# Top-k read: chosen probabilities by exp(scores) minus exp(scores without the chosen), subtracted on GpSimd

## What is computed

```python
# x: (16, 64, 256), the query rows; ctx_1024: (16, 1601, 256), the memory rows
q = query @ Wq.T + bq
k = mem_state @ Wk.T + bk
v = mem_state @ Wv.T + bv
scores = jnp.einsum('btd,bsd->bts', q, k) * scale
vals, idx = jax.lax.top_k(scores, top_k)              # top_k = 32 of s = 1601
masked = jnp.full_like(scores, -jnp.inf)
scores = masked.at[b_ix, t_ix, idx].set(vals)
attn = jax.nn.softmax(scores, axis=-1)
ctx = jnp.einsum('bts,bsd->btd', attn, v)
return ctx @ Wo.T + bo                                # added to x
```

## Time and profile before

| | us |
|---|---|
| median of 3 runs | 1908.88 |
| lowest and highest | 1906.41, 1911.81 |
| the profiled execution, first to last instruction (its span) | 1909.7 |
| TensorE busy in it | 1562.7 |
| VectorE busy | 1234.9 |
| ScalarE busy | 866.1 |
| GpSimd busy | 370.7 |

### The profile page before, as it was taken

One profiled execution on the slowest core, in us unless ns is written; L12 is line 12 of the kernel. 1 busy time (PEld: TensorE's weight loads), 2 busy tenths in 40 slices (PEclk: granted clock), 3 DMA queues, 4 the chain that ended last, 5 costly groups with the idle time before them and its releaser, 6 DMA issues. The chain is left out here.

```text
span 1909.7 us, 32902 instructions
## 1 busy us (share of the span) xinstructions
PE 1562.7 (82%) x11828; PEld 1276.4 (67%) x11828; DVE 1234.9 (65%) x2268; ACT 866.1 (45%) x2127; POOL 370.7 (19%) x444
## 2 busy tenths in 40 slices
PE   7888876679557988988889888888898885649997
PEld 4555554469546877877778778777787773436665
DVE  4999745743554777777777767777678674554443
ACT  2444411220014666656666657566666662123322
POOL 0000000010031344224322432243224000031110
PEclk9777788679858999999999999999999997779999
DMA  9577206005030111011101110111010001020000
GB/s 331 207 278 283 90 1 254 1 1 177 10 123 1 37 37 37 1 38 37 37 2 37 37 38 1 38 37 37 2 37 1 1 1 45 14 118 38 1 1 22
DMA packets 74561, 118.97 MB, mean 62 GB/s; under 512 B 1312, under 2 KB 66976, under 8 KB 73376
## 3 DMA queue, kind: packets, MB, share of 16 engines
q1 hardware_dynamic: 74400, 116.76, 17.4%
HBM read 114.66 MB, written 2.10 MB: 61 GB/s over the span
## 5 line engine op out<-in xcount | busy, mean ns | idle before, releaser
L1535 ACT ACTIVATE d_exps<-psum,d_negmax 128x400 f32<-128x400 f32 (+1 forms) x512 | 297.8, 595 | 37.8 <-DVE d_negmax L1609 35.3
L1436 PE MATMUL psum<-pk,d_exps 128*128 128x128 f32 (+1 forms) x1664 | 265.8, 277 | 20.9 <-DVE d_probT L1619 11.7
L1415 PE MATMUL psum<-d_keys,d_pairq 128*128 128x402 f32 x1024 | 248.8, 376 | 20.6 <-issue 13.2
L1609 DVE TENSOR_REDUCE d_negmax<-psum 128x1 f32<-128x1608 f32 x128 | 234.4, 1831 | 48.4 <-PE psum L1415 46.9
L1646 DVE SCALAR_TENSOR_TENSOR d_keys<-psum,d_bk,d_keys 64x400 fp32r<-64x400 f32 (+1 forms) x256 | 162.4, 634 | 115.5 <-ACT d_keys L1518 108.7
L1313 POOL TENSOR_SCALAR d_rowsN<-d_rowsN,d_rowmoments 128x256 f32<-128x256 f32 x195 | 235.8, 1224 | 0.1
L1436 PEld LDWEIGHTS psum<-pk,d_exps 128*128 128x128 f32 (+1 forms) x1664 | 200.0, 141 | 47.9 <-DVE d_probT L1619 19.8
L1415 PEld LDWEIGHTS psum<-d_keys,d_pairq 128*128 128x128 f32 x1024 | 179.7, 195 | 55.6 <-ACT d_exps L1535 36.4
L1392 PE MATMUL psum<-d_rowsT,d_wk 128*128 128x400 f32 (+1 forms) x768 | 173.8, 362 | 19.6 <-DVE d_keys L1646 18.8
L1619 DVE COPY d_probT<-psum 128x512 f32<-128x512 f32 x256 | 174.0, 687 | 23.7 <-PE psum L1436 19.2
L1543 ACT ACTIVATE d_probT<-psum 128x512 f32<-128x512 f32 x128 | 76.6, 599 | 234.3 <-PE psum L1436 232.8
(11 more groups left out here) (376 smaller groups left out, 2472.0 us busy)
## 6 DMA issues: line engine op xcount, KB each, us to landing
a_cR<-ctx_rows_dram SPq DMA_DIRECT2D x16, 1664.0 KB, 11.6
d_rowsN<-ctx_rows_dram SPq DMA_DIRECT2D x16, 1664.0 KB, 7.8
a_cT<-ctxT_dram SPq DMA_DIRECT2D x16, 1601.0 KB, 14.2
moe_w<-moe_w_dram SPq DMA_DIRECT2D x16, 1024.0 KB, 10.1
f_raw<-trees_dram SPq DMA_DIRECT2D x3, 2048.0 KB, 9.2
pc<-pc_dram SPq DMA_DIRECT2D x1, 1968.0 KB, 11.0
pb<-pb_dram SPq DMA_DIRECT2D x1, 1666.0 KB, 6.7
pd<-pd_dram SPq DMA_DIRECT2D x1, 1164.0 KB, 5.1
```

The costliest lines, as they stand in the source:

```text
L1415: last = pe.matmul(ps[:, c, 0:SCORED], pairq[:, part, m, g, :, :], keys[:, m, g // 2, s0:s0 + SCORED], start=(part == 0), stop=(part == 1))
L1436: last = pe.transpose(ps[0:w, T_BANK + t % 2, (c % 4) * P:(c % 4 + 1) * P], exps[:, p % 2, c * P:c * P + w], core.p("ident"))
L1535: act.activation(exps[:, p % 2, s0:s0 + w], ps[:, c, 0:w], ACT.Exp, bias=negmax[:, p % 2:p % 2 + 1], accum_out=sums[:, p // 4, p % 4, c:c ...
L1609: dve.tensor_reduce(negmax[:, p % 2:p % 2 + 1], ps[:, 0:4, 0:SCORED], XY, ALU.max, negate=True)\
```

## The change

The selection of probabilities is written in another way. `match_replace` leaves LOWEST at the chosen places of `left`, so that exp(left - max) is 0 there and exp(scores - max) everywhere else. ScalarE (`drop`) now writes that exponential into `left` itself, and GpSimd (`keep`) subtracts it from `probs`: the chosen places keep their value, the others become 0. The row's total comes from an exponential of the 32 values in `best`, summed on the way. The pass on VectorE goes. On ScalarE `drop` stands at the head of `take`, and `row_squares(i, u, 0)` moves in front of the copies. `left` now has two more readers, so VectorE waits for `a_gone` and `a_probs` of the pair before ahead of its first `match_replace`, and for `a_total` ahead of the reciprocal.

```diff
--- before.py
+++ after.py
@@ -286,6 +286,7 @@
         fence = core.tensor(ctx, "a_fence", [P, 1])
         total = core.tensor(ctx, "a_total", [P, 2])
         inv = core.tensor(ctx, "a_inv", [P, 2])
+        picked = core.tensor(ctx, "a_picked", [P, TOPK])
         read, readT, valT = xn, xnT, qT
         block = ctx.enter_context(nc.Block())
         T_BANK, V_BANK, SUM_BANK = 4, 6, 7
@@ -301,6 +302,20 @@
         def _(pool):
             pool.memset(ones[:, :], 1.0).then_inc(sig("a_cleared"), 1)
             pool.memset(cstats[:, :, :], 0.0).then_inc(sig("a_cleared"), 1)
+
+            def keep(i, u, first=False):
+
+                n = 2 * i + u
+                pool.wait_ge(sig("a_gone"), n + 1)
+                if not first:
+                    pool.wait_ge(sig("a_probs"), n)
+                pool.tensor_tensor(probs[:, :], probs[:, :], left[:, :], ALU.subtract).then_inc(sig("a_probs"), 1)
+
+            keep(0, 0, first=True)
+            with pool.Fori(1, NT // 2) as i:
+                keep(i - 1, 1)
+                keep(i, 0)
+            keep(NT // 2 - 1, 1)
 
         @block.sync
         def _(sp):
@@ -435,7 +450,7 @@
                 n = 2 * i + u
                 act.wait_ge(sig("a_pair_q"), n + 1)
                 if not first:
-                    act.wait_ge(sig("a_probs"), n - 1)
+                    act.wait_ge(sig("a_left"), 4 * n - 4)
                 for c, (s0, w) in enumerate(QUARTERS):
                     act.wait_ge(sig("a_scores_ps"), 4 * n + c + 1)
                     act.activation(scores[:, u, s0:s0 + w], ps[:, c, 0:w], ACT.Identity,
@@ -482,9 +497,22 @@
                 act.activation(cstats[:, bass.ds((2 * n + j) * NC, SHARE), 2], spread[:, j * SHARE:(j + 1) * SHARE],
                                ACT.Copy).then_inc(sig(f"a_spread{j}"), 1)
 
+            def drop(i, u, first=False):
+
+                n = 2 * i + u
+                act.wait_ge(sig("a_best"), 4 * n + 4)
+                if not first:
+                    act.wait_ge(sig("a_inv"), n)
+                act.activation(picked[:, :], best[:, :, :].rearrange("p r e -> p (r e)"), ACT.Exp, bias=negmax[:, 0:1],
+                               accum_out=total[:, u:u + 1]).then_inc(sig("a_total"), 1)
+                act.wait_ge(sig("a_left"), 4 * n + 4)
+                act.activation(left[:, :], left[:, :], ACT.Exp, bias=negmax[:, 0:1]).then_inc(sig("a_gone"), 1)
+
             def take(i, u, first=False):
 
                 n = 2 * i + u
+                drop(i, u, first)
+                row_squares(i, u, 0, first)
                 for g in range(4):
                     act.wait_ge(sig("a_probsT_ps"), 4 * n + g + 1)
                     if g == 0 and not first:
@@ -495,7 +523,6 @@
                     else:
                         act.activation(probsT[0:SL, 12, :], ps[0:SL, T_BANK + 1, 0:P], ACT.Copy)\
                            .then_inc(sig("a_probsT"), 1)
-                row_squares(i, u, 0, first)
                 act.wait_ge(sig("a_pair_read"), n + 1)
                 act.wait_ge(sig("a_inv"), n + 1)
                 act.activation(read[:, bass.ds(2 * i + u, 1), :].rearrange("p a d -> p (a d)"),
@@ -553,6 +580,8 @@
             def choose(i, u, first=False):
                 n = 2 * i + u
                 dve.wait_ge(sig("a_scores"), 4 * n + 4)
+                if not first:
+                    dve.wait_ge(sig("a_left"), 4 * n)
                 for r in range(TOPK // 8):
                     src = scores[:, u, :] if r == 0 else left[:, :]
                     if r:
@@ -560,17 +589,15 @@
                     dve.memset(fence[:, :], 0.0)
                     dve.max(best[:, r, :], src).then_inc(sig("a_best"), 1)
                     dve.wait_ge(sig("a_best"), 4 * n + r + 1)
+                    if r == 0 and not first:
+                        dve.wait_ge(sig("a_gone"), n)
+                        dve.wait_ge(sig("a_probs"), n)
                     if r == 0:
                         dve.tensor_scalar(negmax[:, :], best[:, 0, 0:1], -1.0, None, ALU.mult)\
                            .then_inc(sig("a_negmax"), 1)
                     dve.memset(fence[:, :], 0.0)
                     dve.match_replace(left[:, :], best[:, r, :], src, LOWEST).then_inc(sig("a_left"), 1)
-                dve.wait_ge(sig("a_left"), 4 * n + 4)
-                dve.wait_ge(sig("a_exp"), n + 1)
-
-                dve.scalar_tensor_tensor(probs[:, :], left[:, :], LOWEST, probs[:, :], ALU.is_le, ALU.mult,
-                                         accum_out=total[:, u:u + 1]).then_inc(sig("a_probs"), 1)
-                dve.wait_ge(sig("a_probs"), n + 1)
+                dve.wait_ge(sig("a_total"), n + 1)
                 if not first:
                     dve.wait_ge(sig("a_read"), n)
                 dve.reciprocal(inv[:, u:u + 1], total[:, u:u + 1]).then_inc(sig("a_inv"), 1)
```

## The result

| | before | changed |
|---|---|---|
| median | 1907.64 us (4 runs) | 1936.55 us (4 runs) |
| lowest and highest | 1904.54, 1911.81 | 1934.97, 1940.97 |
| profiled execution: its time, its span | span 1909.7 | 1936.23, span 1934.4 |
| end of the last value | 231.86 us | 260.18 us |

The change makes the kernel slower: the ratio is 1.0152, 95% interval 1.0132 to 1.0173, which is 28.9 us of the medians. Forecast were 1945 us, a range of 1926 to 1960, and slower with 0.93.

A forecast was written before the change was run, and what follows sets the result against it. VectorE, 97% busy, was taken to bound the kernel before, and a ring through TensorE the changed one. Six turns add 25.8 us and the ends 5.2 each, 36.2 in all: 1945 us, range 1926 to 1960.

The forecast's parts named there:

- The ring: Per turn, score, sums, row_means, drop, GpSimd, transposes and value in sequence through TensorE: 28.2 us against 23.9, chance 0.72.
- GpSimd's price: GpSimd's added subtraction of 128x1601 for each pair, taken as 3.9 us.
- my two slopes: GpSimd's TENSOR_TENSOR from 256 to 1024 columns, 2.59 or 2.23 ns a column: 4.1 or 3.6 us for the subtraction.
- The dear price's rival: GpSimd's subtraction takes 7.65 us in place of 3.9: 30 us more, 1975 us, chance 0.07.
- The ends: First and last pair, where drop, GpSimd and hand-offs delay transposes and value: 5.2 us more each.
- The clock's rival: Slower, but TensorE keeps its full clock in value: 2.3 us less in eight values, 1927 us, chance 0.14.
- The term of 11.9 us: TensorE's transposes and value(n-1) in the ring, read from the last pair's row behind 5.39 us of idle time.
- VectorE and the transfers: Both keep up: VectorE idles over 5 us a turn; 13.0 us of waiting for `cT` become waits for GpSimd.
- The 25.7 us: Transfers' limit: score(n+1) can't start sooner than 25.7 us after value(n-2) ended, which lies under the 28.2 us turn.
- Nothing for row_squares: The moved row_squares on ScalarE, 4 x 0.5 us and more, costs nothing while GpSimd's subtraction takes over 2.4 us.
- Span and time: Converting the profiled span to a median: 1909.7 us plus 36.2 gives 1945.9, with the median 0.8 us lower.
- The faster rival: VectorE's 15 us come through and the turn falls to 22 us: 1894 us, chance 0.04.

The follow-up runs named there:

- The extra matmuls: Changed kernel plus 26, then 21, unread identity matmuls on TensorE between the sums and the wait for the probabilities: 1927.0 and 1926.8 us.
- the two ends mended: The run of 1899.0 us, with the select pass kept on VectorE for the first and the last pair: 1894.1 us (0.9928).
- the run with the copies first: Changed kernel with drop ahead of gather, second row_squares in ScalarE's wait for value, first row_squares back behind the copies: 1899.0 us (0.9958).

## Why the prediction was right

**The ring.** It was summed at 28.2 us and measured at 27.3 in the mean. By parts, from the rows of the turn at 129.78:

| part | summed | measured |
|---|---|---|
| score and sums | 9.3 | 9.2 |
| row_means to its end at 139.80 | 0.8 | 0.8 |
| drop (to 142.09), with 0.35 of issue | 2.1 | 2.3 |
| hand-offs | 0.2 | 0.3 |
| GpSimd | 3.9 | 3.6 |
| transposes and value | 11.9 | 11.7 |
| sum | 28.2 | 27.9 |

The turn itself is 157.43 - 129.78 = 27.65, as the next scores start 0.2 us before value's modelled end. It is the longest of the six; in the turn from 157.43 to 184.56 there is no idle 0.35 us ahead of `a_picked` and it takes 27.1. The mean is 27.3.

**GpSimd's price** was the term most over-sized: 3.57 us where I took 3.9. It lies just under the lower of my two slopes. The Trainium skill's figure in GPSIMD Engine Reference, section 3.1, from which I had estimated 3.5 us, was the better price; the measured 3.57 agrees. Over eight pairs that is 2.6 us. It is 3.55 to 3.60 us in every run that has it, so nothing that VectorE does beside it shows in it: in the changed kernel it took 3.56 us in the first pair, where VectorE was idle for 2.3 us of it, and 3.56 or 3.57 beside the row statistics. The dear price's rival (7.65 us) is out.

**The ends.** I had 5.2 us for each, measured are 75.34 - 71.14 = 4.2 and 21.1 - 17.3 = 3.8. About two thirds of the difference is GpSimd's term and that of transposes and value again (11.5 and 11.3 us in place of 11.9; in the last pair value took 7.53 us). Together: 6 x 3.4 + 4.2 + 3.8 = 28.4 us, against 36.2 summed. These 7.8 us are nearly all of what lies between 1945 and 1936.5.

**The clock's rival** was given 0.14. It did not come true: transposes took 3.13 us and value 7.7 to 8.1 in every turn, and behind the idle time the granted clock was 0.50, half, as these stretches of one turn show (stretch, columns as in the earlier trace rows):

```profile
146.00:149.00 3.00, 3.00 (x13) 2.41 (x13) 2.85 (x7) 1.29 (x3) 0.00 (x0) 0.50 1.02 413
150.00:154.00 4.00, 4.00 (x22) 2.50 (x24) 3.91 (x6) 0.00 (x0) 0.00 (x0) 0.53 0.97 399
154.00:157.00 3.00, 3.00 (x31) 2.15 (x29) 2.91 (x6) 0.00 (x0) 0.00 (x0) 1.00 0.00 0
```

The extra matmuls showed that the turn gets 1.7 us back, net, when TensorE is kept busy (granted clock 0.90 in place of 0.75). But the prediction tied the slow value to the idle time too closely. In the kernel before, value took 7.4 to 8.4 us in seven of eight pairs, and in five of these no idle time ahead of the transposes or of value was longer than 1.01 us. The term of 11.9 us came out right as a reading of the nearest row, and not because the idle time alone explains it.

**VectorE and the transfers** did what was written: VectorE waits 5.0 to 5.8 us before the reciprocal in five turns and 8.1 in the first ("over 5 us"), and there is no wait for `cT`. That the transfers bind once the ring falls below them is shown by the turn of 24.7 and then 23.9 us. The 25.7 us is not one fixed number, though: with the exponentials ahead of row_means, the scores that waited for `cT` start 24.6 to 26.2 us after the value of pair n-2 ended.

**Nothing for row_squares**, covered by GpSimd: right in the changed kernel (1936.9 against 1936.55), and wrong as soon as the cover was gone, as the run with the exponentials ahead of gather found.

**Span and time.** I put the median 0.8 us below the profiled span. The executions here have a time 1.8 us above their span (1936.23 and 1934.4), so the profile of before, at 1909.7, was most likely taken of the longest of its runs, 1911.81. It changes nothing in the sum, which comes to the median plus 36.2 us: 1908.9 + 36.2 = 1945.1.

The faster rival failed for the reason given: the hand-over must be paid between the sums and the transposes. The runs add what the prediction had not worked out, that most of the 15 us were there to be had: VectorE's turn of 21.6 us in place of 23.9, once `drop` stood where `left` becomes ready, and 12.6 us of the whole with the two ends mended.

## What to carry to other kernels

Taking work from the busiest engine helps only if the new chain does not pass through engines whose program order holds it behind something unrelated: write down, for each added instruction, what stands ahead of it in its engine's own order and which engine that one waits for. When a hand-over to other engines costs more latency than the work it removes, it belongs in the steady turns, where other work covers it, and not in the first and the last. And when a wait goes, go through everything that had been hidden beside it.

## What was not expected of the hardware

VectorE's turn fell by 2.3 us (23.9 to 21.6), though the pass that went took 1.83 + 0.08 us. The rest is in how the next instructions start. In the gapless order (the run with the copies first) the reciprocal starts at 99.18, before the MATCH_REPLACE ahead of it has ended (97.45 + 1.81 = 99.26), and the row statistics start 0.07 us after the reciprocal's start. In the kernel before the reciprocal starts at 101.23, 1.9 us after that MATCH_REPLACE ended (97.51 + 1.81 = 99.32), and the statistics 0.26 us after the reciprocal's start, at 101.49.

Value was also slow where TensorE had hardly waited. Value(5) of the kernel before, whose transposes had no idle time ahead of them:

```profile
176.28 3.11 PE L392 MATMUL psum<-pk,a_probs 128*128 128x128 f32 x13
180.22 7.71 PE L403 MATMUL psum<-a_cR,a_probsT 128*64 128x256 f32 x52 [0.82 <-ACT a_probsT L496]
...
182.00:184.00 2.00, 2.00 (x12) 1.30 (x10) 1.96 (x3) 0.18 (x1) 0.00 (x0) 0.50 1.07 410
```

The last line is the busy time of a stretch within it, with 0.50 as the granted clock. In the run with the copies first value took 8.59 and 8.40 us in two turns and 5.83 in two others. It goes the other way too: behind 13.30 us of idle time, in the last pair of the run with the subtraction twice, the transposes took 3.13 us, but value 5.83. What decides between them stays open.
